# Graph layers on one core: the first norm's gain and shift moved to ScalarE, VectorE's 128x4 sums written as scalar-tensor-tensor

## What is computed

```python
for l in range(3):
    si = x @ attn_w[l, :d];  sj = x @ attn_w[l, d:]
    scores = si[:, :, None] + sj[:, None, :] + attn_b[l]
    scores = where(scores >= 0, scores, 0.2 * scores)
    scores = where(mask, scores, -inf)
    agg = einsum('bij,bjd->bid', softmax(scores), x)
    h = layernorm(x + agg, g1[l], beta1[l])          # norm * g1 + beta1
    ff = gelu(h @ W1[l] + b1[l]) @ W2[l] + b2[l]
    x = layernorm(h + ff, g2[l], beta2[l])
```

## Time and profile before

| | |
|---|---|
| median of 3 runs | 1895.2 us (1893.5 to 1897.09) |
| span of the profiled execution | 1892.0 us, mean granted TensorE clock 0.963 |
| DVE, ACT, POOL busy | 1513.0 (80%), 1120.7 (59%), 1314.4 us (69%) |
| PE busy, weight loads busy | 1672.9 (88%), 1482.6 us (78%) |
| chain that ended last, by engine | PE 24%, DVE 20%, POOL 19%, issue 11%, ACT 3% |

### The profile page before, as it was taken

The page is one execution under the profiler, slowest core; times in us unless marked ns, Lnnn a source line. Parts: engine busy times, 40 slices in busy tenths (PEclk is TensorE's granted clock), DMA queues, the critical chain, the costliest instruction groups (busy, mean ns, idle before and its releaser), DMA issues.

```text
span 1892.0 us, 40139 instructions
## 1 busy us (share of the span) xinstructions
PE 1672.9 (88%) x12032; PEld 1482.6 (78%) x12032; DVE 1513.0 (80%) x5366; ACT 1120.7 (59%) x2718; POOL 1314.4 (69%) x1690
## 2 busy tenths in 40 slices
PE   5999999965999999999899999999989898989895
PEld 4777777754888888888788888888878787878784
DVE  3888888877788778788887887887888888888873
ACT  3888888864556556556465565565554545554542
POOL 3355555534787787787777877877868787888786
PEclk8999999996999999999899999999999898999998
DMA  5233333323121121121211211211212122212101
GB/s 181 63 89 89 89 89 89 89 79 123 34 67 58 42 67 58 42 67 54 91 56 44 67 52 47 67 53 47 67 34 68 64 70 65 68 64 69 63 26 45
DMA packets 150477, 127.31 MB, mean 67 GB/s; under 512 B 14880, under 2 KB 143392, under 8 KB 150432
## 3 DMA queue, kind: packets, MB, share of 16 engines
q1 hardware_dynamic: 145024, 124.30, 21.4%
q10 hardware_dynamic: 5408, 2.50, 0.5%
HBM read 89.03 MB, written 37.75 MB: 67 GB/s over the span
## 4 chain that ended last, share of the span: by engine, by line
PE 24%; DVE 20%; POOL 19%; issue 11%; ACT 3%; POOLq 1%; DVEq 0%; ACTq 0%
PE ps L45 14%; PE ps L819 6%; POOL gnn_norm L154 5%; DVE gnn_junk L913 5%; PE ps L795 3%; DVE gnn_small L929 2%; POOL gnn_norm L742 2%; POOL gnn_h L746 2%; POOL xo L761 2%; POOL gnn_norm L757 2%; POOL inv L149 2%; DVE gnn_small L934 2%; DVE gnn_small L937 2%; DVE gnn_res L972 1%; DVE gnn_st L976 1%
## 5 line engine op out<-in xcount | busy, mean ns | idle before, releaser
L819 PE MATMUL ps<-gnn_w_hi,gnn_g_hi 128*128 128x256 f32 x1536 | 454.8, 296 | 41.7 <-DVE gnn_res L972 41.0
L819 PE MATMUL ps<-gnn_w_lo,gnn_g_hi 128*128 128x256 f32 x1536 | 445.7, 290 | 0.0
L819 PE MATMUL ps<-gnn_w_hi,gnn_g_lo 128*128 128x256 f32 x1536 | 444.9, 290 | 0.0
L141 POOL TENSOR_TENSOR fence_pool<-half_neg 128x1 f32<-128x1 f32 x304 | 64.1, 213 | 477.3 <-DVE gnn_mv L1063 169.0
L980 DVE TENSOR_TENSOR gnn_g_lo<-ps,gnn_g_hi 128x512 fp32r<-128x512 f32 x384 | 263.1, 685 | 135.3 <-ACT ps L893 135.2
L892 ACT ACTIVATE gnn_g_hi<-ps,b_cols 128x512 fp32r<-128x512 f32 x384 | 264.5, 689 | 179.4 <-PE ps L45 155.3
L819 PEld LDWEIGHTS ps<-gnn_w_hi,gnn_g_hi 128*128 128x128 f32 x1536 | 305.6, 199 | 47.5 <-DVE gnn_res L972 44.8
L45 PE MATMUL ps<-gnn_hT_hi,gnn_w_hi 128*128 128x512 f32 x768 | 333.4, 434 | 4.0 <-DVE gnn_g_lo L980 4.0
L869 ACT ACTIVATE gnn_e<-gnn_u,gnn_small 128x128 f32<-128x128 f32 x192 | 74.9, 390 | 400.3 <-DVE gnn_small L938 400.3
L819 PEld LDWEIGHTS ps<-gnn_w_lo,gnn_g_hi 128*128 128x128 f32 x1536 | 306.7, 200 | 1.9
L819 PEld LDWEIGHTS ps<-gnn_w_hi,gnn_g_lo 128*128 128x128 f32 x1536 | 305.8, 199 | 0.0
(11 more groups left out here) (116 smaller groups left out, 3925.2 us busy)
## 6 DMA issues: line engine op xcount, KB each, us to landing
hist<-xo SPq DMA_DIRECT2D x48, 512.0 KB, 3.3
x<-hist SPq DMA_DIRECT2D x48, 512.0 KB, 4.3
gmask<-mask_hist SPq DMA_DIRECT2D x48, 256.0 KB, 4.5
aw<-in_L_gnn_attn_w SPq DMA_DIRECT2D x48, 256.0 KB, 4.3
att_xq<-in_x SPq DMA_DIRECT2D x16, 512.0 KB, 4.8
att_xl<-in_x SPq DMA_DIRECT2D x16, 512.0 KB, 3.5
gnn_fin<-hist SPq DMA_DIRECT2D x16, 512.0 KB, 3.8
out<-gnn_fin SPq DMA_DIRECT2D x16, 512.0 KB, 2.8
```

What stands on the lines that cost most here:

```text
L141: e.tensor_tensor(fence_pool[:, n:n + 1], half_neg[:, 0:1], half_neg[:, 0:1], ALU.add)
L819: mm = e.matmul(FF2[j % 2], g[a][:, m, j * N:(j + 1) * N], V[b][:, m, :], start=(n == 0), stop=(n == len(terms) - 1))
```

## The change

ScalarE now multiplies by g1 and adds beta1 on the transposed norm, where features lie on the partitions and both are columns (`g1_cols`, `beta1_cols`, six more loads at the start). Per k it runs an Identity activation into SBUF (the high part) and a second in place in PSUM. POOL normalises into `n1`, which PE transposes in place of h; the sum L746 is gone, and `hb` is made from `n1` in two steps. The wait for the earlier transposes moves from the front of L746 to a fence of its own, ahead of the small steps. On DVE the tensor-scalar and the tensor-tensor instructions of `masked_sums` and `probs_max` become scalar-tensor-tensor.

```diff
@@ -87,6 +87,8 @@
         ps = whole.enter_context(nc.psum_tensor("ps", [P, 8, 512], F32))
         ident = sb("ident", [P, P])
         b1_cols = sb("b1_cols", [P, L, FT])
+        g1_cols = sb("g1_cols", [P, L, KT])
+        beta1_cols = sb("beta1_cols", [P, L, KT])
         affine = sb("affine", [P, L, 5, D])
         b2_rows = sb("b2_rows", [P, L, D])
@@ -299,7 +301,7 @@
                 make_masks(0, 0, 0)
-                e.wait_ge(const_ld, 16 * (5 + L))
+                e.wait_ge(const_ld, 16 * (5 + 3 * L))
                 e.tensor_tensor(affine[:, :, 2, :], affine[:, :, 1, :], b2_rows[:], ALU.add).then_inc(aff_set, 1)
                 def body(q, par, a1, a2):
@@ -474,6 +476,8 @@
                 with nc.allow_non_contiguous_dma(reason="columns of b1, once"):
                     for l in range(L):
                         e.dma_start(b1_cols[:, l, :], b1[l].rearrange("(m p) -> p m", p=P)).then_inc(const_ld, 16)
+                        e.dma_start(g1_cols[:, l, :], g1[l].rearrange("(k p) -> p k", p=P)).then_inc(const_ld, 16)
+                        e.dma_start(beta1_cols[:, l, :], beta1[l].rearrange("(k p) -> p k", p=P)).then_inc(const_ld, 16)
                 for n in range(6):
                     proj_copy(0, 0, n)
                 for k in range(KT):
@@ -737,15 +742,13 @@
                     l = layer_of(t1)
                     hold_pool(e, mv1_out, t1 + 1)
-                    layernorm_on_pool(e, ln1, 6 * t1, mv1, inv, y1, norm)
-                    e.wait_ge(ln1, 6 * t1 + 5)
-                    e.tensor_tensor(norm[:], norm[:], row(l, 0), ALU.mult).then_inc(ln1, 1)
-                    e.wait_ge(ln1, 6 * t1 + 6)
                     if not isinstance(t1, int):
-                        e.wait_ge(hT_made, 2 * t1)
-                    e.tensor_tensor(h[:], norm[:], row(l, 1), ALU.add).then_inc(h_out, 1)
-
-                    e.tensor_tensor(hb[par1][:], norm[:], row(l, 2), ALU.add).then_inc(hb_out, 1)
+                        hold_pool(e, hT_made, 2 * t1)
+                    layernorm_on_pool(e, ln1, 5 * t1, mv1, inv, y1, n1, n1_out)
+                    e.wait_ge(n1_out, t1 + 1)
+                    e.tensor_tensor(hb[par1][:], n1[:], row(l, 0), ALU.mult).then_inc(ln1, 1)
+                    e.wait_ge(ln1, 5 * t1 + 5)
+                    e.tensor_tensor(hb[par1][:], hb[par1][:], row(l, 2), ALU.add).then_inc(hb_out, 1)
                     e.wait_ge(hb_out, t1 + 1)
                 def ln_ffn(t, par, half, last_layer):
@@ -802,10 +805,10 @@
                     mm.then_inc(sjT_made, 1)
                 def transpose_h(t1):
-                    e.wait_ge(h_out, t1 + 1)
+                    e.wait_ge(n1_out, t1 + 1)
                     for k in range(KT):
                         for j in range(GROUP):
-                            mm = e.transpose(HT[k][:, j * N:(j + 1) * N], h[:, j, k * P:(k + 1) * P], ident[:])
+                            mm = e.transpose(HT[k][:, j * N:(j + 1) * N], n1[:, j, k * P:(k + 1) * P], ident[:])
                         mm.then_inc(hT_made, 1)
                 def ffn2(t, j, a2):
@@ -875,9 +878,13 @@
                     e.activation(warm[:, n:n + 1], half_neg[:, 0:1], ACT.Gelu)
                 def hT_hi(t1):
+
+                    l = layer_of(t1)
                     for k in range(KT):
+                        gain, shift = g1_cols[:, bass.ds(l, 1), k], beta1_cols[:, bass.ds(l, 1), k]
                         e.wait_ge(hT_made, 2 * t1 + k + 1)
-                        e.copy(hT[0][:, k, :], HT[k]).then_inc(hT_hi_out, 1)
+                        e.activation(hT[0][:, k, :], HT[k], ACT.Identity, bias=shift, scale=gain)
+                        e.activation(HT[k], HT[k], ACT.Identity, bias=shift, scale=gain).then_inc(hT_hi_out, 1)
                 def body(q, par, a1, a2, layer_end, final):
                     t = 2 * q + par
@@ -926,21 +933,25 @@
                     ins.then_inc(u_out, 1)
                     e.wait_ge(aij_out, t2 + 1)
-                    e.tensor_scalar(small[:, 0, :], s_i[:], ab[par2][:, 0:1], None, ALU.add).then_inc(bias_step, 1)
-                    e.wait_ge(bias_step, 3 * t2 + 1)
+                    e.scalar_tensor_tensor(out=small[:, 0, :], in0=s_i[:], scalar=ab[par2][:, 0:1], in1=zeros[:],
+                                           op0=ALU.add, op1=ALU.add).then_inc(bias_step, 1)
                     e.wait_ge(u_out, t2 + 1)
-                    e.tensor_tensor(small[:, 1, :], top[:], small[:, 0, :], ALU.add).then_inc(bias_step, 1)
+                    e.scalar_tensor_tensor(out=small[:, 1, :], in0=s_i[:], scalar=ab[par2][:, 0:1], in1=top[:],
+                                           op0=ALU.add, op1=ALU.add).then_inc(bias_step, 1)
                     e.wait_ge(bias_step, 3 * t2 + 2)
                     e.scalar_tensor_tensor(out=small[:, 2, :], in0=small[:, 1, :], scalar=0.2, in1=small[:, 1, :],
                                            op0=ALU.mult, op1=ALU.max).then_inc(bias_step, 1)
                     e.wait_ge(bias_step, 3 * t2 + 3)
-                    e.tensor_tensor(small[:, 3, :], small[:, 0, :], small[:, 2, :], ALU.subtract)
+                    e.scalar_tensor_tensor(out=small[:, 3, :], in0=s_i[:], scalar=ab[par2][:, 0:1], in1=small[:, 2, :],
+                                           op0=ALU.add, op1=ALU.subtract)
                     e.scalar_tensor_tensor(out=small[:, 4, :], in0=small[:, 0, :], scalar=0.2, in1=small[:, 2, :],
                                            op0=ALU.mult, op1=ALU.subtract).then_inc(bias_out, 1)
                 def probs_max(t1):
                     e.wait_ge(exp_out, t1 + 1)
-                    e.tensor_tensor(e1[:], e1[:], e2[:], ALU.max).then_inc(p_out, 1)
+                    e.scalar_tensor_tensor(out=e1[:].rearrange("p j n -> p (j n)"), in0=e1[:].rearrange("p j n -> p (j n)"),
+                                           scalar=0.0, in1=e2[:].rearrange("p j n -> p (j n)"),
+                                           op0=ALU.max, op1=ALU.max).then_inc(p_out, 1)
                 def residual1(t1, par1, j):
@@ -1024,7 +1035,7 @@
                     for m in range(FT):
                         gelu_lo(t, m)
                         if a1 and m == 0:
-                            e.wait_ge(h_out, t1)
+                            e.wait_ge(n1_out, t1)
                         if a1 and m < GROUP:
                             residual1(t1, p1, m)
                         if a1 and 1 <= m <= GROUP:
```

More of the change, by code:

```diff
@@ L109, in gnn_kernel @@
         mv_out, ln_chain, ln_out = sems("mv_out", "ln_chain", "ln_out")
-        ident_set, const_ld, w_ld, aff_set = sems("ident_set", "const_ld", "w_ld", "aff_set")
+        ident_set, const_ld, w_ld, aff_set, zeros_set = sems("ident_set", "const_ld", "w_ld", "aff_set", "zeros_set")
         stored = sems("stored_even", "stored_odd")
@@ L596, in gnn_kernel @@
             small = sb("small", [P, 5, GROUP])
+            zeros = sb("zeros", [P, GROUP])
             e1 = sb("e1", [P, GROUP, N])
@@ L603, in gnn_kernel @@
             norm = sb("norm", [P, GROUP, D])
-            h = sb("h", [P, GROUP, D])
+            n1 = sb("n1", [P, GROUP, D])
             hb = [sb(f"hb{i}", [P, GROUP, D]) for i in range(2)]
@@ L620, in gnn_kernel @@
             (w_hi_set, w_split, x_ones, ff1_made, gelu_out, g_lo_out, pT_made, pT_out, agg_made, aij_out, sjT_made,
-             u_out, bias_step, bias_out, exp_out, p_out, recip_out, y1_out, bn1_out, mv1_out, ln1, h_out, hb_out,
+             u_out, bias_step, bias_out, exp_out, p_out, recip_out, y1_out, bn1_out, mv1_out, ln1, n1_out, hb_out,
              hT_made, hT_hi_out, hT_lo_out, ff2_made, y2_out, bn2_out, mv2_out, ln2, norm2_out, x_out) = sems(
@@ L625, in gnn_kernel @@
                     "agg_made", "aij_out", "sjT_made", "u_out", "bias_step", "bias_out", "exp_out", "p_out",
-                    "recip_out", "y1_out", "bn1_out", "mv1_out", "ln1", "h_out", "hb_out", "hT_made", "hT_hi_out",
+                    "recip_out", "y1_out", "bn1_out", "mv1_out", "ln1", "n1_out", "hb_out", "hT_made", "hT_hi_out",
                     "hT_lo_out", "ff2_made", "y2_out", "bn2_out", "mv2_out", "ln2", "norm2_out", "x_out")))
@@ L1074, in _ @@
                 e.sem_inc(y2_out, START)
+                e.memset(zeros[:], 0.0).then_inc(zeros_set, 1)
+                e.wait_ge(zeros_set, 1)
                 for j in range(GROUP):
```

## The result

The changed kernel takes 1940.4 us (median of 4 runs, 1935.5 to 1941.4) against 1894.8 us before (median of 4 runs, one more than above): 2.4% slower (ratio 1.0236, 95% interval 1.022 to 1.0251). The forecast was 1923 us in a range of 1888 to 1951. The profiled executions have spans of 1933.6 and 1892.0 us, 41.6 us apart.

A forecast was written before the change was run, and what follows sets the result against it. The bound was taken as a loop from GpSimd's `mv2` through its sums that block VectorE, then VectorE's work back to `mv2`. Terms +37.5 + 11 - 26 + 5 = +27.5 us on 1895.2 gave 1923 us, range 1888 to 1951.

The forecast's parts named there:

- first two layers without the fall: ScalarE's activations and the second fence lengthen 30 of 32 steps by 1.25 us each: +37.5 us (30 to 43).
- ScalarE's activations: Four activations in place of two copies make `hT_lo` later: +1.05 us a step (0.8 to 1.2).
- fall of TensorE's clock: Longer TensorE idle time ahead of the next body drops its clock in one step of three: +11 us (0 to 33).
- last layer: GpSimd's third sum leaves the loop there: net -2.0 us in 13 steps, -26 us (-30 to -13).
- start: Six more column loads on ScalarE's queue ahead of the copies TensorE waits for: +5 us.
- Do the new sums escape: VectorE's scalar-tensor-tensor sums still wait for GpSimd's sums; first and fourth are held; no gain in the first two layers' loop.
- Rival 2: TensorE's clock falls in every step, 33 us in place of 11: 1945 us; chance 0.2.
- The second fence: GpSimd's extra fence costs 0.27 us a step, less up to 0.04 at two places; taken as +0.2 us.
- the cover of `hT_hi`: In the last layer VectorE's `final_statistics` covers `hT_hi`; if that cover were gone, up to 1.2 us.
- Rivals 3 and 4: Fourth 128x4 sum slips through GpSimd's gap: 1838 us, chance 0.08; new form passes everywhere: 1813 us, chance 0.04.

The follow-up runs named there:

- TensorE kept busy: Changed kernel with five extra 128x256 matmuls, their result unread, on TensorE at the end of each step: 1911.9 us (1.0093).
- plain copies: Changed kernel with ScalarE's four activations replaced by the two copies of before, g1 and beta1 left out of the product's input: 1869.5 us (0.987).
- only its third sum moved: Kernel before, with only GpSimd's third sum (hb) made to wait for `bias_out`: 1857.8 us (0.9813).
- the version behind `bias_out`: Changed kernel with GpSimd's two hb sums waiting for VectorE's 128x4 sums (`bias_out`): 1785.5 us (0.9429); 1781.0 us with the 128x4 operations in their old form.

## Why the prediction was right

The 41.6 us between the two profiled spans fall apart by the starts of bodies, and the two versions that isolate a part give the terms:

| term | forecast | measured | from |
|---|---|---|---|
| first two layers without the fall | +37.5 | +38 | their 32 steps: 923.5 us before, 961.7 us with TensorE kept busy |
| of it ScalarE's activations | +31.5 | +34 | the same 32 steps: 927.5 us with plain copies |
| fall of TensorE's clock | +11 | +27 | 988.3 us in the changed kernel, 961.7 us kept busy |
| last layer | -26 | -27 | its 14 steps: 442.6 and 416.1 us |
| start | +5 | +2 | first probs_T at 432.10 and 434.11 us |
| first graph step | 0 | +1.5 | 22.50 and 23.99 us (22.56 us with plain copies) |

The medians lie 45.5 us apart, 4 us more than these spans. The profiled execution was the fastest of the four (1935.5 us; the others took 1939.7 to 1941.4 us, at a granted clock of 0.956 to 0.957 for 0.958). More falls in them would explain it; no trace shows them.

The prediction had the mechanisms of the first two layers right, one term much too small, and in the last layer its sum came out for reasons that are in part others.

- **Do the new sums escape.** No, as argued from rows 4 and 5. It is the start that decides, for all forms. Of the three forms, rows 3 show only the first two held up; for scalar-tensor-tensor it is rows 4 and 5 that do. The text had the first and the fourth instruction wait; in 18 of 26 steps the third waits in place of the fourth. The second instruction took 0.21 us where 0.15 was assumed, and GpSimd's gap was 0.18 us for 0.22 to 0.26. `bias_out` comes within 0.35 us of the second sum's end either way.
- **ScalarE.** Forecast were 0.59, 0.78 and 0.59 us between the activations; they stand 0.66 us apart, the same sum, and +1.08 us a step (28.64 to 29.71) stands for the +1.05 taken.
- **The clock.** This is the term that was mis-sized, +11 us for +27. The cause was right (2.5 us of idle time, forecast as 2.6), and the price nearly so (27 us over 19 falls in ordinary steps and some at the layer ends, some 1.25 us each, for 1.1). The share was not: "a fall in one step of three" was a guess between no fall and a fall always, and it was 19 of 26. Rival 2, with a fall in every step, gave 1945 us; the measured 1940 lies nearer to it than to the forecast. Rows 7 and 8 had idle stretches of 1 us without a fall and of 2.7 us with one, and the new one lies between, near the upper end: that should have weighed more.
- **The second fence.** Taken at +0.2 us a step. Without it nothing that could be measured came back in the device time. In the traces like steps are 0.1 to 0.3 us shorter without it, but more of them have a fall. That the new form costs 0.1 us a step was not in the sum.
- **The last layer.** -2.14 us a step for -2.0, a hit that is in part luck. As forecast, L942 waits for the second sum and nothing waits for a third. Two things were not in the sum. The falls of this layer went, but for one: the last `ffn2` block took 4.5 us (1532.38 to the next body at 1536.87) and takes 3.1 us now. And the cover of `hT_hi`, counted as kept, is gone: TensorE idles 1.30 to 1.45 us ahead of probs_T, behind the activations and the low parts. The first works for the change and the second against it, and no run separates them from the third sum. The kernel before with only its third sum moved gains from the same two places: its granted clock is 1.00 there too.
- **The start.** Less than half of the +5 us taken. The kernels with the six column loads have their first probs_T at 432.5 to 436.0 us, those without at 431.7 to 432.1, so the term is 2 to 3 us and scatters as much.
- **Rivals 3 and 4** had 0.12 between them and did not come. Their picture of what would follow, a step bound by TensorE at 26.6 to 27.2 us, is what the version behind `bias_out` shows (26.8 us), by another way.

## What to carry to other kernels

When one engine's long SBUF operations hold another's short ones up, rewriting the short ones in another form was worth nothing here; ask when each has to start, and put the long ones behind the short ones. Here the changed kernel lost 2.4% by moving work from GpSimd to ScalarE, where the chain then ran, and one more wait turned the same work into a gain of 6%. A step that gets longer by idle time of TensorE costs that time and, where the clock falls, a good part of it again (here 38 us and 27 us more); a stretch of useless matmuls measures that second part by itself.

## What was not expected

- The turn at the gap is exact to hundredths: the third 128x4 instruction passed where it started together with GpSimd's sum by the profile, and was held for 2.38 us where it started 0.01 us later. In the changed kernel 8 of 26 steps are of the first kind and 18 of the second. A schedule that relies on such a gap is not safe.
- VectorE holds GpSimd up as well: GpSimd's 128x1024 sum took 2.37 us alone, 2.66 us behind probs_max and 3.31 us behind final_sum. The Trainium skill (SBUF — State Buffer, Who interferes with whom) has it that the order of issue, not the form of the operation, decides who is blocked; the trace agrees in both directions, as in the last two cases VectorE's instruction had started 0.30 and 0.16 us earlier. The expectation for the sums behind `bias_out` had used only the direction in which VectorE waits.
- In the profiled executions, the kernel without the second fence has 25 of 26 steps with a fallen clock, for 19 with it, and so gives back what it gains in each. Which steps fall isn't explained by the idle time ahead of them.
